# Experts' first layer in a transformer kernel: weights held in TensorE, copied there by VectorE, result with channels in partitions

## The reference, cut to what matters

```python
B, T, S_ENC, D, H, E, K = (4, 128, 64, 128, 16, 8, 2)
HID = 4 * D
...
topk_vals, topk_idx = jax.lax.top_k(logits, K)
topk_gates = jax.nn.softmax(topk_vals, axis=-1)
...
h = jnp.einsum('nd,ehd->neh', xf, exp_w1)      # first layer of the experts
h = jax.nn.silu(h)
eo = jnp.einsum('neh,edh->ned', h, exp_w2)     # second layer
sel = jnp.einsum('ned,ne->nd', eo, gates)
return (sh + sel).reshape(b, s, d)
```

## Time and profile before

| | |
|---|---|
| time, median of 3 runs | 770.46 us (768.5 to 770.67) |
| the profiled execution's own time | 768.48 us |
| its span, first to last instruction | 766.7 us |
| mean granted TensorE clock | 0.958 of full speed |
| PE, PEld busy | 696.0 us (91%), 465.6 us (61%) |
| DVE, ACT, POOL busy | 532.0 us (69%), 447.1 us (58%), 316.5 us (41%) |
| the blocks' first and last PE record | start 470.8 us and 569.1 us |

### The profile page before, as it was taken

The page is one execution under the profiler, slowest core; times in us unless marked ns, Lnnn a source line. Parts: engine busy times, 40 slices in busy tenths (PEclk is TensorE's granted clock), DMA queues, the critical chain, the costliest instruction groups (busy, mean ns, idle before and its releaser), DMA issues.

```text
span 766.7 us, 26376 instructions
## 1 busy us (share of the span) xinstructions
PE 696.0 (91%) x9248; PEld 465.6 (61%) x9248; DVE 532.0 (69%) x1306; ACT 447.1 (58%) x1242; POOL 316.5 (41%) x523
## 2 busy tenths in 40 slices
PE   2999999999999999999998598999964789999996
PEld 1556666767666666666665366777742456666774
DVE  0688888788898877778887431444422588888884
ACT  1376666676766777777665333433412556667874
POOL 2244444466666533333575730433332144443110
PEclk9999999999999999999999699999995699999997
DMA  8343333222323211111110011121214001011110
GB/s 258 89 93 73 90 79 89 65 64 52 106 77 107 82 29 33 31 37 29 42 45 23 29 33 25 48 54 52 53 31 134 19 19 36 26 31 36 47 38 25
DMA packets 60044, 44.59 MB, mean 58 GB/s; under 512 B 18073, under 2 KB 54429, under 8 KB 58800
## 3 DMA queue, kind: packets, MB, share of 16 engines
q1 hardware_dynamic: 53152, 25.95, 12.6%
q10 hardware_dynamic: 4528, 13.18, 7.0%
q0 software_dynamic: 2272, 4.24, 1.7%
HBM read 22.72 MB, written 14.79 MB: 49 GB/s over the span
## 4 chain that ended last, share of the span: by engine, by line
PE 70%; issue 14%; POOL 6%; DVE 3%; ACT 3%; DMA 2%; ACTq 1%; SPq 0%; POOLq 0%; DVEq 0%
PE ps L565 11%; PE ps L607 10%; PE ps L787 5%; PE ps L727 5%; PE ps L797 5%; PE ps L583 4%; PE ps L660 4%; PE ps L735 4%; PE ps L648 3%; PE ps L682 3%; POOL k_by_j L495 2%; PE ps L592 2%; PE ps L755 2%; PE ps L807 2%; PE ps L661 2%
## 5 line engine op out<-in xcount | busy, mean ns | idle before, releaser
L1080 DVE TENSOR_REDUCE top<-ps 128x16 f32<-128x1024 f32 (+1 forms) x96 | 108.9, 1134 | 63.1 <-PE ps L565 62.1
L487 POOL TENSOR_TENSOR rstd<-spread,half_neg 128x1 f32<-128x1 f32 x80 | 44.5, 556 | 208.3 <-DVE spread L1172 122.9
L495 POOL TENSOR_TENSOR k_by_j<-k_t,cst 128x512 f32<-128x512 f32 (+1 forms) x96 | 95.3, 992 | 81.3 <-ACT k_t L904 44.9
L565 PE MATMUL ps<-k_by_j,q_t 32*64 32x256 f32 (+1 forms) x1536 | 124.0, 393 | 0.3
L607 PE MATMUL ps<-cst,prob 128*128 128x128 f32 x704 | 118.9, 289 | 0.8 <-ACT prob L925 0.7
L607 PEld LDWEIGHTS ps<-cst,prob 128*128 128x128 f32 x704 | 76.1, 142 | 60.3 <-issue 57.0
L1095 DVE TENSOR_TENSOR prob<-ps,top 128x1024 f32<-128x1024 f32 (+1 forms) x96 | 108.9, 1134 | 0.7
L925 ACT ACTIVATE prob<-prob 128x1024 f32<-128x1024 f32 (+1 forms) x96 | 94.8, 987 | 20.8 <-DVE prob L1095 19.7
L1046 DVE RECIPROCAL inv<-ps 128x128 f32<-128x128 f32 x96 | 91.6, 954 | 11.6 <-PE ps L735 7.5
L874 ACT ACTIVATE prob_t<-ps 128x512 f32<-128x512 f32 (+1 forms) x96 | 53.9, 561 | 45.0 <-PE ps L607 44.7
L872 ACT ACTIVATE prob_t<-ps 128x512 f32<-128x512 f32 (+1 forms) x96 | 53.9, 561 | 42.0 <-PE ps L607 39.4
(11 more groups left out here) (157 smaller groups left out, 1271.5 us busy)
## 6 DMA issues: line engine op xcount, KB each, us to landing
sorted_rows<-zero_rows ACTq DMA_DIRECT2D x32, 276.2 KB, 2.7
stage_x<-x_t SPq DMA_DIRECT2D x80, 64.0 KB, 1.8
mow<-in_mow SPq DMA_DIRECT2D x18, 256.0 KB, 3.1
stage_kv<-in_ctx_t SPq DMA_DIRECT2D x64, 64.0 KB
stage_m<-in_m SPq DMA_DIRECT2D x80, 32.0 KB
rows_in<-sorted_rows SPq DMA_DIRECT2D x39, 65.0 KB, 1.9
wat<-in_wat ACTq DMA_DIRECT2D x1, 1280.0 KB, 6.4
stage_x<-in_x_t SPq DMA_DIRECT2D x16, 64.0 KB, 1.9
```

The lines of the kernel that those rows point to most:

```text
L495: pool.tensor_tensor(k_by_j[:, p, 0:nj, :], k_t[:, p:p + 1, :].broadcast_to([128, nj, TOK]), cst[:, cj:cj + nj].unsqueeze(2).broadcast_to( ...
L565: mm = pe.matmul(ps[S * b:S * b + S, 2 * p + bank, r * nj * S:(r + 1) * nj * S].rearrange("p (h k) -> p h k", k=S), q_t[rows_g, p, S * b:S ...
L1080: dve.tensor_reduce(top[:, p, 0:nh].rearrange("p (b h) -> p b h", b=2), sc, AX.X, ALU.max).then_inc(top_d, 1)
```

## The change

The first layer's roles are exchanged. The expert's weights become the stationary matrix, in four pieces of 128x128, and the tokens stream past each of them. The result of the four matmuls has the hidden channels in partitions, which is the layout that the second layer wants, so Silu writes `hid_t` directly. The four transpositions, their PSUM banks and the copy L1267 are gone. The stationary matrix is read from a fixed buffer here: DVE reads the expert's number to a register of its own and copies that expert's 512 columns of `mow1` to `first_w[j % 2]`.

```diff
-        hid = sb("hid", [128, 2, HID])
+        first_w = sb("first_w", [128, 2, HID])
         hid_t = sb("hid_t", [128, 2, HID])
...
@@ PE
-                for s in range(NB + 3):
+                for s in range(NB + 2):
...
                         pe.transpose(ps[:, B_XT[j % 2], 0:128], rows_in[:, j % LOOK, 0:D], ident).then_inc(b_xt, 1)
-                    j = s - 1
-                    if 0 <= j < NB:
-                        pe.wait_ge(b_xs, j + 1)
-                        if j >= 2:
-                            pe.wait_ge(b_act, j - 1)
-                        pe.matmul(ps[:, B_H[j % 2], :], rows_t[:, j % 2, :],
-                                  mow1[:, bass.ds(expert[j], 1), :].rearrange("k e h -> k (e h)"), start=True, stop=True)\
-                            .then_inc(b_h, 1)
-                    j = s - 3
+                    j = s - 2
                     if j >= 0:
-                        pe.wait_ge(b_te, j + 1)
+                        pe.wait_ge(b_act, j + 1)
                         if j >= 2:
                             pe.wait_ge(b_y, j - 1)
...
-                    j = s - 2
+                    j = s - 1
                     if 0 <= j < NB:
-                        pe.wait_ge(b_act, j + 1)
+                        pe.wait_ge(b_w, j + 1)
+                        pe.wait_ge(b_xs, j + 1)
                         if j >= 2:
-                            pe.wait_ge(b_te, j - 1)
+                            pe.wait_ge(b_act, j - 1)
                         for c in range(HC):
-                            mm = pe.transpose(ps[:, B_HT[j % 2], c * 128:(c + 1) * 128], hid[:, j % 2, c * 128:(c + 1) * 128], ident)
-                        mm.then_inc(b_t, 1)
+                            mm = pe.matmul(ps[:, B_H[j % 2], c * 128:(c + 1) * 128],
+                                           first_w[:, j % 2, c * 128:(c + 1) * 128],
+                                           rows_t[:, j % 2, :], start=True, stop=True)
+                        mm.then_inc(b_h, 1)
@@ ACT
-                            act.wait_ge(b_t, j - 1)
-                        act.activation(hid[:, j % 2, :], ps[:, B_H[j % 2], :], ACT.Silu).then_inc(b_act, 1)
+                            act.wait_ge(b_acc, j - 1)
+                        act.activation(hid_t[:, j % 2, :], ps[:, B_H[j % 2], :], ACT.Silu).then_inc(b_act, 1)
@@ DVE
+                dve.wait_ge(n_t, 1)
+                for s in range(NB + 2):
+                    j = s
+                    if j < NB:
+                        e = dve.value_load(weight_of[0:1, j:j + 1], min_val=1, max_val=E)
+                        if j >= 2:
+                            dve.wait_ge(b_h, j - 1)
+                        dve.tensor_copy(first_w[:, j % 2, :], mow1[:, bass.ds(e, 1), :].rearrange("k e h -> k (e h)")).then_inc(b_w, 1)
+                    j = s - 2
                     if j >= 0:
                         dve.wait_ge(b_acc, j + 1)
...
-                        dve.wait_ge(b_t, j + 1)
-                        if j >= 2:
-                            dve.wait_ge(b_acc, j - 1)
-                        dve.tensor_copy(hid_t[:, j % 2, :], ps[:, B_HT[j % 2], :]).then_inc(b_te, 1)
```

More of the change, by code:

```diff
@@ L241, in build @@
         B_SH, B_SY = (0, 1), (2, 3)
-        B_XT, B_H, B_HT, B_Y = (0, 1), (2, 3), (4, 5), (6, 7)
+        B_XT, B_H, B_Y = (0, 1), (2, 3), (6, 7)
         loaded = {k: sem(f"loaded_{k}") for k in ("small", "x_tok", "rows", "wat", "ff", "l3", "order", "mo")}
@@ L282, in build @@
         s_h, s_act, s_acc, s_res = (sem(f"s_{k}") for k in ("h", "act", "acc", "res"))
-        b_xt, b_xs, b_h, b_act, b_t, b_te, b_acc, b_y = (
-            sem(f"b_{k}") for k in ("xt", "xs", "h", "act", "t", "te", "acc", "y"))
+        b_xt, b_xs, b_w, b_h, b_act, b_acc, b_y = (
+            sem(f"b_{k}") for k in ("xt", "xs", "w", "h", "act", "acc", "y"))
         ld_rows = [sem(f"ld_rows{p}") for p in range(LOOK)]
@@ L1253, in blocks @@
             def blocks():
-                for s in range(NB + 1):
-                    j = s - 1
+                dve.wait_ge(n_t, 1)
[7 more added lines that the diff above has]
+                    j = s - 2
                     if j >= 0:
@@ L1261, in blocks @@
                                           ALU.mult).then_inc(b_y, 1)
-                    j = s
-                    if j < NB:
-                        dve.wait_ge(b_t, j + 1)
-                        if j >= 2:
-                            dve.wait_ge(b_acc, j - 1)
-                        dve.tensor_copy(hid_t[:, j % 2, :], ps[:, B_HT[j % 2], :]).then_inc(b_te, 1)
             def combine(k):
```

## The result

The changed kernel takes 784.03 us (median of 4 runs, 782.19 to 786.56) against 770.57 us (4 runs, 768.5 to 771.13). The ratio is 1.0177, 95% interval 1.0153 to 1.0201: slower, by 1.5 to 2.0%. The profiled execution took 785.65 us, with a span of 783.8 us and a mean clock of 0.956.

The account below looks back on a forecast made before the run. The kernel before was taken as bound by a PE and DVE loop, 2.45 us per block. A new loop of 2.80 over 38 blocks, less 1.45 at the start, adds 11.8 us: 780.3 profiled, 781 forecast, range 776 to 788.

Parts of the forecast that it names:

- The loop: PE and ACT per block: second layer, first layer and Silu in series without overlap, 2.80 us against 2.45; chance 85%.
- its rivals: Array sets the pace, 750 us, 6%; clock falls, near 846, 5%; scatter becomes the bound, 790, 2%; no change, 2%.
- The old loop: Kernel before: second layer and transpositions on PE, copy on DVE, next second layer; 2.45 us per block, array time 2.27.
- The cover: DVE's weight copy (0.22 to 0.69 us) and register read, PE's transposition and register work: hidden, adding nothing to the step.
- Start and end: Around the blocks: first second-layer load 1.45 us earlier at 473.56, last at 579.96, so the blocks end 11.8 us later.
- The clock: PE rests 0.97 us in every 2.80; at 1.2 GHz through all blocks 66 us more, near 846; chance 5%.
- 1.00 through the blocks: Sign expected in the profile after: PE's granted clock stays at 1.00 through the blocks.
- The rival on the other side: PE's array sets the pace in the blocks: 2.0 us per block, 750 us, faster; chance 6%.

Follow-up runs that it names:

- the second set: Runs on one chip; here the kernel before with transpositions ahead of the second layer and the copy ahead of the gate's multiplication: 757.95 us, ratio 0.9913.
- the third set: Runs on one chip: changed kernel with five filling transpositions in its first three steps 782.71 us, in all steps 782.3 us, and unedited 783.45 us.
- the first experiment: Changed kernel with the first layer of one block put ahead of the second layer of the block before it on PE: 743.79 us, ratio 0.9697.

## Why the prediction was right

**The loop.** This was the step that carried the forecast, and it held. The terms after, against those summed: 0.89 and 0.89 from weight load to weight load, 0.11 and 0.11, 1.06 and 1.05, 0.03 and 0.03, 0.60 and 0.60, 0.13 and 0.12. The step is 2.82 us, not 2.80. Four experiments tell it from its rivals: opened, the step is 1.90; shortened by splitting Silu, 2.22; with 0.21 us less Silu, 2.61; with neither copy nor register load on DVE, 2.82.

**The old loop.** That the kernel before was paced by its own loop and not by its nearly full array was read from the drain, and the second set showed it: 2.30 us when opened.

**The cover.** DVE's work, the transposition and PE's register work cost nothing, as said. The copy is 0.43 us, between the bounds of 0.22 and 0.69. DVE's register reads, bounded by PE's 0.68, are 0.31 + 0.19 + 0.06 us. The scatter's lengthening, for which one copy's length was the bound, 0.69, is 0.18.

**Start and end.** 2.79 us from the first transposition to the first second layer; the forecast had 473.56 - 470.77 = 2.79. That the last second layer would start at 579.96 and the blocks end near 581 did not hold: it started at 588.58, 2.7 later for the late start, 0.7 for the step, 5.2 for the clock.

**The clock.** Its rival was costed for all blocks and given 5%. What happened is a part of it, in the first blocks only: 5.2, 5.3 and 1.7 us in the three profiles. So the sign "1.00 through the blocks" failed. The forecast looked for evidence in the drain, where PE comes from 90 us of dense work; the place to look was the start, where PE had rested 1.8 us just ahead. The rows of before could not have shown it: its first transposition stands behind the same rest, 1.74 us against 1.77, as PE's rows before and after say, and its clock stays at 1.00:

```profile
470.78 0.32 PE L781 MATMUL ps<-cst,rows_in 128*128 128x128 f32 x1 [1.74 <-issue]
```

```profile
473.45 0.32 PE L781 MATMUL ps<-cst,rows_in 128*128 128x128 f32 x1 [1.77 <-issue]
```

What differs is the work behind that rest. The fall at the start is the term that was left out. What it does to the median is not settled: the third set puts it near 1 us, with intervals that overlap.

**The number.** 781 was forecast and 784.03 measured, 13.5 us above before by the medians, where 11.8 had been summed. The step's 0.02 accounts for 0.8 of the difference. The profiled executions are 17.1 apart, and there the late start (2.7) and the clock's fall (5.2), which weren't in the sum, are offset in part by 3.3 us behind the blocks. So the loop, which makes 12.6 us of it net of the shorter start (14.0 - 1.45), was foreseen; that the rest stayed inside the range is in part luck, since the range was made for other terms. Beside before, the changed kernel was 13.5, 15.8 and 13.6 us slower in the three comparisons that were made.

**The rival on the other side**, the array as the pace at 2.0 us per block and 750 us, was rejected for this order and is true of the other order: 1.90 and 743.8.

## What to carry to other kernels

Work taken from a nearly full engine is worth nothing if the new order closes a longer loop; write the loop down before and after (what must follow what without overlap, with the hand-offs) and compare it with the engine's own time. When stages are merged, re-space the pipeline: an engine's next group should belong to a block whose input was started one whole group earlier. Here the same work took 1.018 times the time of the kernel before with the second layer directly behind its own block's Silu, and 0.970 times with another block's first layer put between.

## What the runs showed of the hardware

- A float32 copy of 128x512 within SBUF takes DVE 0.427 us, against 0.691 us for the same size from PSUM.
- Such a copy beside a scatter of POOL's own queue lengthens the scatter's record from 0.98 to 1.16 us. In the first experiment, where it ends 0.06 us into the scatter, the record stays at 0.98. The Trainium skill (SBUF — State Buffer, "SBUF: two separate sides") has GpSimd locked out while such a copy runs; the trace agrees in kind, but the scatter lost only 0.18 us where the copy ran on for 0.31 us beside it.
- In the first blocks of the changed kernel the clock fell from 1.00 to 0.50 for 13, 13 and 7 us in its three profiles, although PE's records covered more than two thirds of that time. The same duty later, once the clock was up, left it at 1.00 for 90 us. Five transpositions of the identity in each of the first three steps kept it up in the profiles. PE had rested 1.8 us just ahead, but so it had in the kernel before, whose clock stayed at 1.00; so the rest alone isn't the cause, and which property of the work behind it is, no run separates. The Trainium skill (TensorE: Matmul & The Clock Gate, "What's actually happening") has the half rate as what activity lifts; the trace agrees in that the clock came back while PE worked.
- With Silu split, ACT read the result of the second of four matmuls 0.71 us after the group began, 0.08 later than the 0.60 of four records and a hand-off of 0.03 would give; the last of the four is read 0.03 us after its record's end.
